# A fused pre-norm block on one core: the first norm of the tokens two sequences ahead, on ScalarE instead of VectorE

## The reference

```python
# x: (16, 512, 512) float32: 16 sequences of 512 tokens, 512 features each
x = x + attention(layernorm(x))   # mLSTM with 8 heads: q, k, v, input and forget gates,
                                  # soft cap 15, a scan over the tokens, a norm per head, a sigmoid gate, Wout
x = x + ffn(layernorm(x))         # 512 -> 2048 -> 512, ternary weights, exact GELU

def _layernorm(x, axis=-1, eps=1e-05):
    m = jnp.mean(x, axis=axis, keepdims=True)
    v = jnp.var(x, axis=axis, keepdims=True)
    return (x - m) / jnp.sqrt(v + eps)
```

## Time and profile before

| | |
|---|---|
| median of 3 executions | 1822.63 us (1822.6 to 1822.96) |
| profiled execution, its own time | 1821.85 us |
| profiled execution, span | 1820.1 us |
| TensorE busy | 1772.3 us, 97% |
| VectorE busy | 1400.6 us, 77% |
| ScalarE busy | 1096.2 us, 60% |
| GpSimd busy | 632.3 us, 35% |
| chain that ended last | PE 90%, DVE 3%, ACT 1%, issue 1% |
| mean granted TensorE clock | 0.985 of full speed |

### The profile page before, as it was taken

The page is one execution under the profiler, slowest core; times in us unless marked ns, Lnnn a source line. Parts: engine busy times, 40 slices in busy tenths (PEclk is TensorE's granted clock), DMA queues, the critical chain, the costliest instruction groups (busy, mean ns, idle before and its releaser), DMA issues.

```text
span 1820.1 us, 31959 instructions
## 1 busy us (share of the span) xinstructions
PE 1772.3 (97%) x12524; PEld 878.3 (48%) x12524; DVE 1400.6 (77%) x2434; ACT 1096.2 (60%) x1815; POOL 632.3 (35%) x481
## 2 busy tenths in 40 slices
PE   5779999999999999999999999999999999999999
PEld 3464444444444444444444444444444444444455
DVE  6786896968779686886968688696878969685772
ACT  5867648375673838557383754738476483745733
POOL 1232342524334251432525243352423425242340
PEclk8869999999999999999999999999999999999999
DMA  8424035251412525042251603325150332414020
GB/s 284 171 87 136 15 84 112 53 143 24 142 31 53 142 48 148 18 126 53 54 142 38 158 13 108 77 53 143 36 147 14 95 101 53 120 24 125 1 53 24
DMA packets 233525, 156.97 MB, mean 86 GB/s; under 512 B 195088, under 2 KB 199312, under 8 KB 228256
## 3 DMA queue, kind: packets, MB, share of 16 engines
q1 hardware_dynamic: 231792, 151.79, 31.5%
q10 hardware_dynamic: 1584, 3.15, 0.5%
HBM read 90.48 MB, written 17.24 MB: 59 GB/s over the span
## 4 chain that ended last, share of the span: by engine, by line
PE 90%; DVE 3%; ACT 1%; issue 1%; POOL 0%; DMA 0%; POOLq 0%; DVEq 0%; ACTq 0%
PE pf L1955 23%; PE pf L1971 23%; PE pa L1820 19%; PE pa L1796 9%; PE psh L1820 6%; PE psh L1911 2%; PE psh L1899 1%; PE psh L1879 1%; PE pa L1787 1%; PE psh L1945 1%; PE psh L1861 1%; PE psh L1834 1%; ACT dec L931 0%; DVE kT L1457 0%; DVE ktok L1423 0%
## 5 line engine op out<-in xcount | busy, mean ns | idle before, releaser
L1971 PE MATMUL pf<-w2T,gT 128*128 128x512 f16 x2048 | 502.3, 379 | 0.0
L1955 PE MATMUL pf<-x2T,w1T 128*128 128x512 f16 x1920 | 427.4, 379 | 0.0
L1511 DVE SCALAR_TENSOR_TENSOR gT<-g,wscale,gT 128x512 f16<-128x512 f32 x240 | 224.0, 933 | 212.8 <-ACT gT L967 210.8
L1955 PEld LDWEIGHTS pf<-x2T,w1T 128*128 128x128 f16 x1920 | 181.6, 98 | 216.2
L1971 PEld LDWEIGHTS pf<-w2T,gT 128*128 128x128 f16 x2048 | 195.3, 97 | 174.8
L1820 PE MATMUL pa<-wT,xT 128*128 128x512 f16 x960 | 213.5, 380 | 1.0 <-ACT sig L890 0.9
L964 ACT ACTIVATE g<-pf,b1c 128x512 f32<-128x512 f32 x240 | 164.3, 685 | 83.0 <-PE pf L1955 77.9
L972 ACT ACTIVATE ktok<-kT 128x512 f32<-128x512 f32 x64 | 40.4, 631 | 237.5 <-DVE kT L1435 237.5
L1820 PE MATMUL pa<-wT,shared 128*128 128x512 f16 x768 | 178.2, 382 | 0.7 <-DMA shared<-qT 0.7
L967 ACT ACTIVATE gT<-g,wscale 128x512 f16<-128x512 f32 x240 | 173.2, 722 | 7.8
L1796 PE MATMUL pa<-xT,wT 128*128 128x512 f16 x768 | 171.3, 379 | 0.1
(11 more groups left out here) (229 smaller groups left out, 2747.0 us busy)
## 6 DMA issues: line engine op xcount, KB each, us to landing
dec<-gate_r SPq DMA_DIRECT2D x32, 1024.0 KB, 5.7
xin<-L_attn_x SPq DMA_DIRECT2D x16, 1024.0 KB, 5.5
out<-x1b SPq DMA_DIRECT2D x64, 256.0 KB, 2.2
xres<-L_attn_x SPq DMA_DIRECT2D x16, 512.0 KB, 5.9
xres<-L_attn_x SPq DMA_DIRECT2D x32, 256.0 KB, 2.9
qw<-gate_w SPq DMA_DIRECT2D x128, 48.0 KB, 5.7
gT<-L_ffn_w SPq DMA_DIRECT2D x5, 1024.0 KB, 4.8
gT<-L_ffn_w ACTq DMA_DIRECT2D x3, 1024.0 KB, 6.2
```

What stands on the lines that cost most here:

```text
L1511: nc.vector.scalar_tensor_tensor(gT[:, LO, f, :], g32[:, f % 2, :], wscale[:, W_GELU:W_GELU + 1], gT[:, HI, f, :], ALU.mult, ALU.subtract) ...
L1955: last = nc.tensor.matmul(bank, w1T[:, k, tok(f)], x2T[:, part, :, k, :], start=(k == 0 and part == HI), stop=(k == KD - 1 and part == LO))
L1971: last = nc.tensor.matmul(bank, gT[:, part, f, tok(t)], w2T[:, f, :], start=(f == 0 and part == HI), stop=(f == NF - 1 and part == LO), sk ...
```

## The change

ACT applies the norm of sequences 2 to 15 with an activation of the form `Identity(scale * x + bias)`, with a scale and a bias for each row: `xrstd` and `xbias` = -`mean` * `xrstd`. POOL writes the reciprocal deviation of these sequences into a tensor of its own, `xrstd`. DVE computes `xbias` at the place where it normalized tiles 0 and 1, and no longer normalizes tiles 2 and 3. ACT's four instructions stand at the end of its order for sequence `b`, ahead of `gates(b + 1)`. Sequences 0 and 1 are normalized by DVE as before.

```diff
@@ gpsimd
             def layer_norm(b):
                 pool.wait_ge(var1, at(b, 1, 1))
-                nc.gpsimd.tensor_tensor(rstd[:, :], ve[:, :], half[:, 0:T], ALU.pow).then_inc(rstd1_ok, 1)
+                nc.gpsimd.tensor_tensor((rstd if b < 2 else xrstd)[:, :], ve[:, :], half[:, 0:T], ALU.pow).then_inc(rstd1_ok, 1)
@@ scalar
+            def tokens_norm(b):
+
+                act.wait_ge(xbias_ok, b - 1)
+                for t in range(T):
+                    nc.scalar.activation(xin[:, t, :], xin[:, t, :], ACT.Identity, bias=xbias[:, t:t + 1],
+                                         scale=xrstd[:, t:t + 1]).then_inc(xn_ok, 1)
...
                 gated_hi(b, 3)
                 between((7,), (5,))
                 between((), (6, 7))
+                if b + 2 < B:
+                    tokens_norm(b + 2)
@@ vector
-                def next_norm(*tiles):
+                def next_bias():
                     if b + 2 < B:
-                        norm_apply(b + 2, tiles)
+                        dve.wait_ge(rstd1_ok, at(b + 2, 1, 1))
+                        nc.vector.scalar_tensor_tensor(xbias[:, :], mean[:, :], -1.0, xrstd[:, :],
+                                                       ALU.mult, ALU.mult).then_inc(xbias_ok, 1)
...
                 residual(b, 1, ca)
-                next_norm(0, 1)
+                next_bias()
                 residual(b, 2, ca)
                 if ahead:
                     gate_sum(b + 1)
-                next_norm(2, 3)
-                if ahead:
                     gate_minus(b + 1)
```

More of the change, by code:

```diff
@@ L172, in block_program @@
         mean, dif, dev, ve, rstd = (sb(n, [P, T]) for n in ("mean", "dif", "dev", "ve", "rstd"))
+        xrstd, xbias = sb("xrstd", [P, T]), sb("xbias", [P, T])
         den, hsum, hvar, hinv = (sb(n, [P, NH]) for n in ("den", "hsum", "hvar", "hinv"))
@@ L250, in block_program @@
         xn_ok, xn2_ok = sem("xn_ok"), sem("xn2_ok")
+        xbias_ok = sem("xbias_ok")
         x_hi, x2t_hi = sem("x_hi"), sem("x2t_hi")
```

## The result

The changed kernel takes 1825.68 us at the median of 20 executions (1824.25 to 1827.85); the kernel before takes 1822.76 us at the median of 20 beside it. The ratio is 1.0014, with a 95% interval of 1.0008 to 1.0021: a loss of about 2.6 us, clear of zero. The forecast's sum was 1.85 us; 1825.68 lies near the upper end of the 1823.5 to 1825.8 that the forecast gave itself. The profiled execution has a span of 1823.5 us against 1820.1.

The account below looks back on a forecast made before the run. The prediction took TensorE (PE) to bound the kernel. Added PE waits, 1.45 us in the turn into sequence 1 and 0.4 over 13 steady turns, sum to 1.85, taking the median from 1822.63 to 1824.5 us; range 1822.5 to 1830.

Parts of the forecast that it names:

- gain 0: DVE, 14 turns: removing 0.56 + 1.49 us ahead of `residual(b, 2)` and two passes under tanh gains nothing.
- 0.44 us in my sum: ACT, steady turns: the copy of the gates could start at 788.60 in place of 788.16, 0.44 us late.
- 5.01 us of idle time: ACT ahead of the copy of the gates: this idle time was said to hide 4.57 us of work and waiting.
- My lower end: PE at `stack`: 0.37 us to spare if the weight load must end before the product needs it.
- The upper end: PE at `stack`: 0.50 us to spare if the product may follow the load's start at once.
- 0.03 us a steady turn: 13 steady turns: PE waits 0 to 0.07 us at `stack`, taken as 0.03, times 13 = 0.4 us.
- every bank was covered: A delay of 0.44, or 2 us in sequence 1, leaves covered every bank that ACT frees.
- the prediction's own signs of being wrong: `xbias` over 1 us, activations longer than 0.81 us, or PE waiting elsewhere than at `stack`.
- rival 1: ACT: each activation, or the four's start, some tenths later; copy 0.84 late, sum 7.1 us, 1829.7; chance 0.16.
- Rival 2: POOL's second tile is served before `xbias`; copy 1.84 late, PE waits 18.3 us in 13 turns, 1842.3; chance 0.08.
- Rival 3: Nothing reaches PE: activations at 0.53 us, or more cover in the first turn; 1822.6 to 1823.4; chance 0.17.
- rival 4: Faster: freed 2.05 us of DVE start something PE waits for earlier; at most some 2 us, 1820.6; chance 0.03.

Follow-up runs that it names:

- experiments 2: Changed kernel with sequences 2 to 15 normalized by no engine, DVE still computing `xbias`; ratio to the kernel before 0.9992 (0.9984 to 1.0001).
- experiment 4: Changed kernel with ACT's four activations spread over its idle times behind the copy of the gates; ratio to the kernel before 0.9993 (0.9984 to 1.0002).
- experiments 5: Changed kernel with three tiles normalized on ACT and the fourth on DVE under tanh; ratio to the kernel before 0.9998 (0.9988 to 1.0007).
- experiment 7: Changed kernel with ACT's copy of the first key half moved behind the last two exponentials; ratio to the kernel before 1.0001 (0.9991 to 1.0010).
- 9: Kernel before with DVE's norm of tile 1 moved behind the residual of tile 2, no norm on ACT; ratio to the kernel before 0.9990 (0.9981 to 0.9999).
- number 3: Changed kernel with one of the two waits of the gates' copy moved ahead of the four activations; ratio to the kernel before 1.0024 (1.0015 to 1.0033).
- number 6: Changed kernel with a fifth activation of the same shape ahead of the four, its output unread; ratio to the kernel before 1.0064 (1.0049 to 1.0079).
- number 10: Changed kernel with a plain 128x512 copy behind the four activations, its output unread; ratio to the kernel before 1.0049 (1.0033 to 1.0064).

## Why the prediction was right, point by point

**What bounds the kernel.** TensorE does, and the change could only make it wait. That held, but "gain 0" for the work taken from DVE was wrong by 0.06 us a turn: experiments 2, 4, 5, 7 and 9 all show it, and 9 shows that it is the bank freed by the residual of tile 2. I had read only the waits of the products. The weight loads' list had it, and so had the products' start at 788.11, right behind the residual's end at 788.05.

**The activation.** 0.80 us alone and 0.71 each in a row were right: four took 2.93 us from the first start to the last end. The lateness, 0.44 us in my sum, measured 0.56. `xbias` ended where I put it; the missing 0.12 are the overlap of the gates' copy that never came (0.10) and its 0.02 behind the end. The remark that the 5.01 us of idle time hide 4.57 us is a slip: they hold 2.61 us of waiting for `xbias` and 2.84 of work, of which 0.44 stick out.

**What TensorE has to spare at `stack`.** Lateness less loss, with the 0.06 us given back at the other bank, is 0.56 - 0.18 = 0.38 in the change, 0.64 - 0.25 = 0.39 in number 3, 1.27 - 0.89 = 0.38 in number 6 and 1.09 - 0.70 = 0.39 in number 10. My lower end was 0.37, and I had taken the middle. That this end came so near is luck in its parts. I had 0.05 us from the end of `stack`'s last part to the load and 0.14 from the load to the product; measured are 0.12 and 0.03 (808.64, 808.76, 808.79). That leaves 0.41, and the products behind start 0.03 later, which makes 0.38. (The upper end, 806.25 - 805.74, is 0.51 and not 0.50.) The copy's lateness and the room together make the term that was mis-sized: 0.03 us a steady turn, 0.4 in all, where 0.18 were lost at `stack` and 0.06 gained at the bank, 0.12 a turn and 1.55 in all. The mechanism in the steady turns was the right one, as experiments 5, 6 and 7 show: remove one activation or give `stack` more room and the loss is gone, add one and all of it is paid.

**The turn into sequence 1.** 1.45 us predicted, 1.53 measured. But the step that led there failed in its place. I said that TensorE waits at `stack`, and that every bank was covered. It waits at the output projection of the last tile, for the bank that the gate sum frees; experiment 7 shows that `stack` costs nothing in this turn. A wait elsewhere than at `stack` was one of the prediction's own signs of being wrong, and it came; for the steady turns it had named under 0.1 us at `stack`, where 0.18 were lost. I had checked the banks that ACT frees and not the one that DVE frees right behind ACT's copy. The number came out by luck, because both places happen to have about the same room here: 2.50 - 1.53 = 0.97 us at the bank, and 0.96 by my reckoning at `stack`.

**The rivals.** Of rival 1 (some tenths later, 1829.7) a part came: the copy was 0.56 us late, short of the 0.6 at which this rival was to decide, and the measured loss lies at most a quarter of the way from the forecast's 1.85 us to its 7.1. Experiment 6 shows that lateness beyond the room is paid in full. Rival 2 did not come: `xbias` got through between POOL's two tiles (0.30 us) in 13 turns, and took 0.60 once, in the turn into sequence 1, where nothing waited for it. Rival 3 did not come; experiment 4 is the kernel in which nothing reaches TensorE. Of rival 4, the faster one, 0.8 us are real, and they are inside the result.

**The sum.** Predicted 1.45 + 0.4 = 1.85 us. Measured 1.53 + 13 x 0.12 = 3.1 us in the traces, 2.6 us by the ratio. The ratio's interval, 1.5 to 3.8 us, holds both 1.85 and 3.1, so the timing alone does not tell that the steady term was off by a factor of nearly four; the traces do.

## What to carry to other kernels

Work moved off a busy engine must land in a gap of the other engine that is long enough. Here the gap ahead of a chain's first instruction was the costly one, since what exceeded it ran through the whole chain: the same four activations cost 3.1 us ahead of the gates and nothing some microseconds later. When one instruction becomes late, follow each of its consumers, and the buffers that the next engine frees behind it, not only the one that looks tightest. Where the bounding engine shows no waits, read its weight loads' waits too, and compare the start of one recurring instruction across two traces: steps of 0.06 us a turn, far below what the timing resolves, stand out there because they recur in each of 13 turns.

## What the runs showed of the hardware

- An activation of 128x512 float32 with both a scale and a bias per row takes 0.80 us, one without them 0.60 to 0.63, and each further one in a row adds 0.71.
- The copy of 40 rows from PSUM into `th` did not overlap with the instruction ahead of it (0.01 to 0.03 us behind its end wherever it stood directly behind one, in eight kernels), while activations and a plain copy over 128 rows did (0.09). One wait ahead of it in place of two changed nothing; the reason is open.
- A VectorE piece over 128x4 (`xbias`) took 0.30 us in 13 turns and 0.60 in one. Both times it began inside a GpSimd tile over 128x512 and ended 0.02 to 0.03 us after that tile (788.19 behind 788.16, 140.93 behind 140.91), so its length tells how early in the tile it began. In the 13 turns a second GpSimd tile followed directly and did not hold it.
- From the end of the instruction that TensorE waited for to its first product it took 0.15 us both at `stack` and at the bank of the gate sum (0.12 to the weight load, 0.03 more to the product).
- The time up to the second sequence's gate products, some 142 us, varied by up to 2.9 us between kernels of the same instructions up to there or nearly so. Why is open.
